# A three-layer transformer block on one core: the order of gathers, stacks and spreads in the transfer queue, and the normalisation chain of layer 2 cut into four parts

## Time and profile before

| | |
|---|---|
| median of three runs | 2903.46 us |
| the profiled execution, span / its own time | 2911.7 us / 2913.56 us |
| layer 1, eight batches | about 74 to 828 us of the span |
| layer 2, eight batches | about 924 to 1768 us |
| MLP | about 1798 us to the end |
| TensorE (PE) busy | 2655.8 us, 91% |
| VectorE (DVE) busy | 1586.8 us, 54% |
| ScalarE (ACT) busy | 1335.7 us, 46% |
| GpSimd (POOL) busy | 644.9 us, 22% |
| mean granted TensorE clock | 0.964 |

### The profile page before, as it was taken

How to read it: one execution, slowest core, us unless ns; L and a number is a source line. 1 busy time by engine, 2 the same in 40 slices (tenths; PEclk the granted TensorE clock), 3 DMA queues, 4 the chain that set the end, 5 groups by cost and what they waited for, 6 DMA issues and landing times. The chain is left out here.

```text
span 2911.7 us, 40922 instructions
## 1 busy us (share of the span) xinstructions
PE 2655.8 (91%) x13584; PEld 2030.4 (70%) x13584; DVE 1586.8 (54%) x4310; ACT 1335.7 (46%) x2755; POOL 644.9 (22%) x528
## 2 busy tenths in 40 slices
PE   5999999999758999999999884999999999999998
PEld 3777767776536666666666653888888888888886
DVE  3777777777635777777787763322222333333333
ACT  2677777767633666666666663211111221111111
POOL 5455555556321122222212111000000000000000
PEclk8999999999868999999999996999999999999999
DMA  5455655555535546455455534211111221111100
GB/s 134 98 139 139 143 119 136 133 138 126 139 85 131 115 101 141 105 112 134 115 108 125 113 62 141 88 45 45 45 45 45 79 90 45 46 45 45 45 29 29
DMA packets 173898, 276.44 MB, mean 95 GB/s; under 512 B 29204, under 2 KB 53524, under 8 KB 173076
## 3 DMA queue, kind: packets, MB, share of 16 engines
q1 hardware_dynamic: 170772, 260.58, 37.2%
q0 software_dynamic: 2304, 12.58, 1.2%
q10 hardware_dynamic: 640, 1.05, 0.1%
HBM read 97.04 MB, written 42.99 MB: 48 GB/s over the span
## 5 line engine op out<-in xcount | busy, mean ns | idle before, releaser
L2235 DVE TENSOR_TENSOR c_product<-c_up_ps,c_gate 128x512 f32<-128x512 f32 x128 | 88.7, 693 | 654.2 <-PE c_up_ps L2301 654.2
L2289 PE MATMUL c_gate_ps<-c_h_split,c_w_split 128*128 128x512 f32 x1536 | 381.2, 397 | 24.5 <-DVE c_w_split L2187 24.5
L2273 PE MATMUL c_down_ps<-c_w_split,c_product_split 128*128 128x512 f32 x1536 | 379.3, 396 | 0.0
L2301 PE MATMUL c_up_ps<-c_h_split,c_w_split 128*128 128x512 f32 x1536 | 378.1, 394 | 0.0
L2289 PEld LDWEIGHTS c_gate_ps<-c_h_split,c_w_split 128*128 128x128 f32 x1536 | 289.6, 189 | 96.9 <-issue 26.3
L2301 PEld LDWEIGHTS c_up_ps<-c_h_split,c_w_split 128*128 128x128 f32 x1536 | 288.0, 188 | 70.5
L2273 PEld LDWEIGHTS c_down_ps<-c_w_split,c_product_split 128*128 128x128 f32 x1536 | 288.5, 188 | 69.0
L279 ACT ACTIVATE b_prob_hi<-b_scores_t_ps 128x384 fp32r<-128x384 f32 (+1 forms) x384 | 200.2, 521 | 224.3 <-PE b_scores_t_ps L270 203.6
L2159 ACT ACTIVATE c_gate<-c_gate_ps 128x512 f32<-128x512 f32 x128 | 76.4, 597 | 494.0 <-PE c_gate_ps L2296 494.0
L287 DVE TENSOR_TENSOR a_prob_lo<-a_scores_t_ps,a_prob_hi 128x384 fp32r<-128x384 f32 (+1 forms) x384 | 225.6, 594 | 138.7 <-ACT a_scores_t_ps L280 136.8
L287 DVE TENSOR_TENSOR b_prob_lo<-b_scores_t_ps,b_prob_hi 128x384 fp32r<-128x384 f32 (+1 forms) x384 | 226.3, 594 | 126.1 <-ACT b_scores_t_ps L280 124.9
(11 more groups left out here) (206 smaller groups left out, 4870.7 us busy)
## 6 DMA issues: line engine op xcount, KB each, us to landing
a_q_stack<-a_q_split SPq DMA_DIRECT2D x192, 128.0 KB, 3.6
a_k_stack<-a_k_split SPq DMA_DIRECT2D x192, 128.0 KB, 3.7
b_q_stack<-b_q_split SPq DMA_DIRECT2D x192, 128.0 KB, 3.3
b_k_stack<-b_k_split SPq DMA_DIRECT2D x192, 128.0 KB, 3.7
c_h_stage<-h_t SPq DMA_DIRECT2D x16, 1024.0 KB, 6.1
c_res<-x SPq DMA_DIRECT2D x16, 1024.0 KB, 5.5
c_w_stage<-in_mlp_w POOLq DMA_DIRECT2D x16, 768.0 KB, 4.5
stage<-in_x_t SPq DMA_DIRECT2D x8, 1024.0 KB, 6.4
```

The lines of the kernel that those rows point to most:

```text
L2235: dve.tensor_tensor(product[:, bank, :], up_ps[:, bank, :], gate[:, bank, :], ALU.mult).then_inc(product_done, 1)
L2273: mm = pe.matmul(down_ps[:, t, :], product_split[:, kt % 2, a, t * P:t * P + P], w_split[:, w, kt, 2 * KC * P:], start=(kt == 0 and i == 0 ...
L2289: pe.matmul(gate_ps[:, bank, :], w_split[:, w, ft, c * 2 * P:c * 2 * P + P], h_split[run.pair][:, a, c, :], start=(c == 0 and w == 0 and a ...
L2301: mm = pe.matmul(up_ps[:, bank, :], w_split[:, w, ft, c * 2 * P + P:(c + 1) * 2 * P], h_split[run.pair][:, a, c, :], start=(c == 0 and w = ...
```

## The change

In layer 1's queue at g = 1 `send_b` comes ahead of the gather; at g = 0 the load comes behind it. `spread` is cut into `spread_out` (to DRAM) and `spread_in` (back); stack pair 0 comes between them, in every step, and pair 1 still comes behind the store. The 12 matmuls of `low` go 2, 3, 3, 4 to slots 1 to 4 instead of 3, 3, 3, 3. In layer 2 `spread_in` follows pair 0 at g = 3 only, and there GpSimd does the sum of `merge` ahead of the chunks, and the rest (`weigh`) behind them. The normalisation chain is cut: `variances` ahead of the low part of unit 9, start and first round of the root behind it, rounds two and three behind the low part of unit 10.

```diff
+LOW_ITEMS = (range(0, 2), range(2, 5), range(5, 8), range(8, 12))
...
             def step(b, g):
                 last = is_last(b)
+                first = isinstance(b, int) and b == 0 and g == 0
+                if g == 1 and not last:
+                    send_b(b + 1)
+                if not first:
+                    gather(*group(b, g, -1))
                 if g == 0 and not last:
                     load(b + 1)
-                first = isinstance(b, int) and b == 0 and g == 0
-                if not first:
-                    gather(*group(b, g, -1))
                 if g == 1 and not last:
-                    send_b(b + 1)
                     send_low(b + 1)
                 if not first:
-                    spread(*group(b, g, -1))
+                    spread_out(*group(b, g, -1))
                 if not (last and g >= 2):
                     stack_send(sp, at, *group(b, g, 2), 0)
                 if not first:
+                    spread_in(*group(b, g, -1))
                     store(*group(b, g, -1))
                 if not (last and g >= 2):
                     stack_send(sp, at, *group(b, g, 2), 1)
...
-                        low(b + 1, share(3 * KC, LOW_SLOTS[1] - LOW_SLOTS[0], slot - LOW_SLOTS[0]))
+                        low(b + 1, LOW_ITEMS[slot - LOW_SLOTS[0]])
...  (layer 2, SyncE)
                 if not first:
-                    spread(*group(b, g, -1))
+                    spread_out(*group(b, g, -1))
+                if g < 3 and not first:
+                    spread_in(*group(b, g, -1))
...
                 if not (last and g >= 2):
                     stack_send(sp, at, *group(b, g, 2), 0)
+                if g == 3:
+                    spread_in(*group(b, g, -1))
...  (layer 2, GpSimd)
+                    if not (isinstance(b, int) and b == 0 and g == 0):
+                        merge(*group(b, g, -1))
                     if g == 3 and has(b, 2):
                         for c in range(KC):
                             attn_chunk(b + 2, c)
                         adapter(b + 2)
                     if not (isinstance(b, int) and b == 0 and g == 0):
-                        merge(*group(b, g, -1))
+                        weigh(*group(b, g, -1))
...  (layer 2, VectorE)
                 for slot in range(UNITS):
+                    if g == 1 and slot == 10 and not last:
+                        variances(b + 1)
                     if slot > 0:
                         lo_unit(dve, at, b, g, slot - 1)
...
                         if slot == 10:
-                            norm_factors(b + 1)
+                            root_start(b + 1)
+                            root_round(b + 1, 0)
                         if slot == 11:
+                            for i in range(1, 3):
+                                root_round(b + 1, i)
                             normalise_tile(b + 1, 0)
                             normalise_tile(b + 1, 1)
```

More of the change, by code:

```diff
@@ L547, in gather, with spread_out @@
                 sp.dma_start(sums[:, :], at.pv_raw[2 * HD:2 * HD + 1, :, :]).then_inc(at.gathered, 16)
-            def spread(b, g):
+            def spread_out(b, g):
                 n = number(b, g)
@@ L553, in spread, with spread_in @@
                 sp.dma_start(sums_hbm.rearrange("h (c n) -> (h c) n", c=TT), inverse[:, :]).then_inc(inverse_out, 16)
+            def spread_in(b, g):
+                n = number(b, g)
                 sp.wait_ge(inverse_out, n * 16 + 16)
@@ L613, in _ @@
             gather(BATCH - 1, GROUPS - 1)
-            spread(BATCH - 1, GROUPS - 1)
+            spread_out(BATCH - 1, GROUPS - 1)
+            spread_in(BATCH - 1, GROUPS - 1)
             store(BATCH - 1, GROUPS - 1)
@@ L1121, in rsqrt, with rsqrt_start @@
 def rsqrt(dve, step, done, out, x, t):
+    rsqrt_start(dve, step, done, out, x, t)
+    for i in range(3):
+        rsqrt_round(dve, step, done, out, x, t, i)
+def rsqrt_start(dve, step, done, out, x, t):
     dve.tensor_scalar(t.bitcast(I32), x.bitcast(I32), 1, None, ALU.logical_shift_right).then_inc(step, 1)
@@ L1125, in rsqrt, with rsqrt_round @@
     dve.tensor_scalar(out.bitcast(I32), t.bitcast(I32), -1.0, RSQRT_MAGIC, ALU.mult, ALU.add).then_inc(step, 1)
[L1126 to L1132, removed]
+def rsqrt_round(dve, step, done, out, x, t, i):
+    dve.wait_ge(step, done + 2 + 3 * i)
+    dve.tensor_tensor(t, out, out, ALU.mult).then_inc(step, 1)
+    dve.wait_ge(step, done + 3 + 3 * i)
+    dve.scalar_tensor_tensor(out=t, in0=t, scalar=-0.5, in1=x, op0=ALU.mult, op1=ALU.mult).then_inc(step, 1)
+    dve.wait_ge(step, done + 4 + 3 * i)
+    dve.scalar_tensor_tensor(out=out, in0=t, scalar=1.5, in1=out, op0=ALU.add, op1=ALU.mult).then_inc(step, 1)
 RSQRT_STEPS = 11
@@ L1630, in add_residual, with variances @@
                 dve.bn_stats(stats[:, t, :], res[:, t, :]).then_inc(stats_done, 1)
-            def norm_factors(b):
+            def variances(b):
                 done = b * LN_STEPS
@@ L1745, in _ @@
                 add_residual(0, t)
-            norm_factors(0)
+            variances(0)
+            root_start(0)
+            for i in range(3):
+                root_round(0, i)
             for t in range(TT):
```

13 lines of the change are left out of this document (10 added, 3 removed).

## The result

| | before | after |
|---|---|---|
| median | 2903.84 us (4 runs, 2903.44 to 2905.91) | 2946.23 us (4 runs, 2944.09 to 2948.30) |
| profiled execution, span | 2911.7 us | 2946.4 us |
| layer 1, from its first to layer 2's first step | 849.8 us | 897.8 us |
| layer 2, from its first step to its last batch | 743.0 us | 728.6 us |

The ratio is 1.0144 (1.0127 to 1.0162). The forecast was 2948. The direction, the place and the size in layer 1 are as forecast (+48.1 for +53); layer 2 gave 14.4 back in these two profiles, where 6.6 was forecast. Between the medians lie 42.4 us, between the two profiled spans only 34.7: the profiled execution of the kernel before lay 10 us above its median, that of the changed kernel 2 us.

What follows compares the result with a forecast made beforehand. SyncE's serial queue bounds layer 1's interval g = 3 to 0, not TensorE. Layer 1 +53 and layer 2 -6.6 make +46 on 2913.56; carried to the median 2949.9, taken as 2948 us, range 2896 to 2970 (own range 2922 to 2968).

Steps and rivals of the forecast that it cites:

- Layer 1's chain: Layer 1: SyncE's queue sets the pace from reciprocal to reciprocal; plain chain 23.9 us, 100.5 a batch, layer +53.
- ScalarE's wait for `wo`: Layer 1, batch 7: weight loads stand behind pair 1, so this wait of 5.37 grows by some 2.5 us.
- The load: Layer 1, interval g = 3 to 0: load of x (2.69 us) leaves the chain as pair 0's 4.13 comes in.
- the step 2 to 3: Layer 1, reciprocals of g = 2 to g = 3: TensorE alone needs 21.01 us; forecast 23.9 after, +2.9.
- The stacks: Layer 1, interval 0 to 1: `send_b` ahead of the gather counts in the chain, 2.2 us; interval +2.7.
- the clock joins in: Rival 3, layer 1: waits lower TensorE's granted clock, 1.5 us a batch (+10); 2975 us; chance 0.08.
- one of my signs: Layer 1, sign that the forecast is right: TensorE below 90% busy.
- The norm chain: Layer 2: 0.76 us gained, 1.15 where TensorE waited for unit 9; 0.95 by 7 batches, -6.6, bounds -1 and -9.
- Two terms at nothing: Layer 1's 2-3-3-4 split of `low`, costed at 0; layer 2's queue at g = 3, 0, at most 0.5 a batch.
- hidden steps: In the sum: 2949.9 us taken as 2948, since steps that wait for pair 1 hide some.

Runs made afterwards that it cites:

- half the cut: Kernel before with layer 1's spread cut, only pair 0's three q transfers ahead of `spread_in`, the three of k behind it: 2928.12 us, ratio 1.0064.
- the heaps: Layer 2 times of the profiled kernels: seven with the old norm chain, 735.6 to 743.0, mean 739.0; seven with the new, 726.7 to 731.7, mean 728.8.

## Why the forecast was right, and where it was not

- **Layer 1's chain: right.** The gather, the copy into `pv_raw` and the reciprocal run at the pace of SyncE's queue. Intervals 26.49, 26.31, 23.56, 23.73 for 26.1, 26.6, 23.9, 23.9; a batch 100.1 for 100.5. Batches 1 to 6 cost +39.2 for +42, batch 0 +3.2 for +4.5, batch 7 and the weights behind it +5.6 for +6.5: +48.1 for +53. ScalarE's wait for `wo` is 8.18 where 5.37 stood, +2.8 for +2.5:

```profile
805.87 0.63 ACT L720 ACTIVATE w_split<-stage 128x512 fp32r<-128x512 f32 x1 [8.18 <-DMA stage<-in_wo_t]
```

- **The step that costs is the cut: shown**, twice, by taking it alone (+60.8) and by leaving it out (0.9946). Its size goes by the issues ahead of `spread_in`, less the wait for the landing in DRAM that they cover, as half the cut shows; the forecast had both. The load was priced rightly within the chain (2.69; 3 to 0 is 26.82 with the cut alone and 23.73 in the changed kernel), but without the cut it is worth only 1.5, since TensorE needs 22.4 there and not the 21 that I took from the step 2 to 3. The stacks cost 1.96 in the queue and only where pair 1 is late; alone they cost 0.
- **A wait that the forecast leaves out.** The gather also waits for the store's landing. In the changed kernel this is covered by pair 1's issues, so the sum came out right without it; the store on GpSimd brought it to light.
- **Where the saved wait went.** TensorE no longer waits for pair 0 (10.6 us), and it comes back as waits for pair 1 (13.4) and, behind ScalarE's wait for the gather, for the low part (17.2 before, 33.3 after, over batches 1 to 6).
- **The clock: a rival that came in part.** I gave 0.08 to "the clock joins in" and had nothing of it in the sum. The clock did fall: of the 24 steps of batches 1 to 6 one ran below 1.00 before, nine after, all six at g = 1 (0.88 to 0.94) and three at g = 3 (0.93). One of them in windows of 2 us, and the wait before it:

```profile
510.00:512.00 2.00, 1.83 (x10) 1.49 (x11) 2.00 (x8) 2.00 (x5) 1.67 (x2) 0.78 0.00 0
512.00:514.00 2.00, 2.00 (x8) 1.38 (x7) 2.00 (x7) 0.64 (x2) 0.00 (x0) 0.50 0.10 28
514.00:516.00 2.00, 2.00 (x13) 1.38 (x12) 1.45 (x6) 1.12 (x3) 0.00 (x0) 0.86 0.51 125
```

```profile
509.94 0.44 PE L268 MATMUL a_scores_t_ps<-a_q_stack,a_k_stack 114*128 114x384 f32 x1 [1.64 <-DVE a_prob_lo L287]
```

  The granted clock falls to 0.50, 1.2 of 2.4 GHz, right behind the wait. Most of the 18 us of additional busy time can be this: a mean clock of 0.97 over 600.56 us is 17 to 18 us of full clock. It does not show in the time, because the chain sets the pace and slower matmuls lie within it. At 1 to 2, over batches 0 to 6 of the changed kernel and of the one with low parts 3-3-3-3, nine intervals with a lower clock have a mean of 26.3 (25.82 to 27.30), and five at 1.00 have 26.3 too (26.07 to 26.71). Where TensorE sets the pace it shows at once: 24.77 for 23.18 to 23.76 at 0 to 1 of the kernel before. So the 1.5 us a batch that this rival put on the clock did not come. This part is read from the traces; no run held the clock and left the waits. It also broke one of my signs: TensorE was to be below 90% busy, and is 90.2% (541.64 of 600.56).
- **The norm chain: right in kind, under-sized.** -10.2 for -6.6, outside my bounds of -1 and -9 by a little. At g = 1 it is -1.17 a batch, -8.2 in all, and that is inside them: I had 0.76 as the rule and 1.15 as the exception, and the 1.15 is the rule. The other 2 us lie at g = 2 and are within what the heaps scatter.
- **Two terms at nothing**, the low parts and layer 2's queue: both measured as nothing; that the split of the low parts guards a wait doesn't show in any run.
- **The sum.** +48 - 10 = +38, where the forecast has +46: layer 1 5 too much, layer 2 4 too little gain. Measured are 42 (1.0144) and, for the all but equal kernel with low parts 3-3-3-3, 38 (1.0131). With the measured terms the same carrying-over gives 2913.56 + 38 - 10.1, about 2941, 5 us under the measured 2946. The forecast's 2948 is 2 above it, with two errors of one sign, 9 us together (less 2 that I took off for hidden steps), that the interval of the ratio (37 to 47 us) hides. That the total came within 2 us is luck; that it lies in the range is not.

## What to carry over

Follow one chain through the reciprocal, or whatever marks a step, from mark to mark through every queue, and compare the sum with the distance: if it fills it, an issue put ahead in that queue is paid in full, less any wait of the queue that it fills; if not, first the slack. What stands behind a wait in an in-order queue is delayed by all that the wait is delayed by; so put independent transfers behind the last thing that the chain needs (as the load), not ahead of it (as pair 0). A gain read off a single profile of before should be checked against other profiles that have the same code: 4 of the 14 us of layer 2 were such. And check all that a transfer waits for: here the gather needed the store's landing too, which only shows when the issues between them are gone.

## What was not expected of the hardware

- The price of an issue varies: pair 1 took 4.35 to the next issue in the earlier trace rows and 3.86 in the changed kernel; three issues mostly take 1.9, and single groups go to 2.5. What makes them longer isn't shown. The number of transfers still under way does not tell: in batches 1 to 6 of the kernel before one issue of a stack takes 0.64 us on average with five of them under way and 0.67 with one.
- The same store took 2.0 us from issue to landing in the changed kernel (median), where nothing had been issued for 3 us or more before it, and 3.4 in the kernel before, where pair 0's issues end just ahead of it.
- The length of a wait of TensorE alone does not tell whether the clock falls to 0.50 behind it. In the changed kernel it fell behind one of 1.64 us. In the kernel before it did not fall behind any of the six waits for pair 0, 1.43 to 2.13 us long, but it did once behind a wait of 1.17 (batch 3, g = 1), where five others of 1.17 or 1.18 were followed by 1.00.
- A transfer issued by GpSimd keeps it for 0.58 us, 0.30 after its multiply; on SyncE the same store's issue takes 0.34, 0.03 to 0.04 after the multiply's end (548.17 for 546.85 + 1.29).
